# Gathering layer 1's target rows in layer 1's own stage, and reading the edge lists first

## The reference

```python
h = jnp.maximum(_layernorm(x, axis=-1), 0.0)
x = x + _L0_gnn_ref(h, src, dst, ...)   # three mean-aggregating layers
...                                     # then L1, L2 and L3 in the same form

def _sage_mean(h, src, dst, inv_deg, W_neigh, W_self, b_self):
    neigh_sum = jax.ops.segment_sum(h[src], dst, num_segments=h.shape[0])
    return h @ W_self.T + b_self + (neigh_sum * inv_deg) @ W_neigh.T
```

## Time and profile before

| | us |
|---|---|
| median of 3 executions (5771.94 to 5776.87) | 5776.05 |
| the profiled execution | 5786.49 |
| its span (first to last instruction) | 5784.8 |
| setup, up to the stage "positions" | 0 to 203.5 |
| "positions" and "lookup" | 203.5 to 738.6 |
| stage A | 738.6 to 1289.5 |
| stage B1 | 1289.5 to 1462.3 |

### The profile page before, as it was taken

How to read it: one execution, slowest core, us unless ns; L and a number is a source line. 1 busy time by engine, 2 the same in 40 slices (tenths; PEclk the granted TensorE clock), 3 DMA queues, 4 the chain that set the end, 5 groups by cost and what they waited for, 6 DMA issues and landing times. The chain is left out here.

```text
span 5784.8 us, 105438 instructions
## 1 busy us (share of the span) xinstructions
PE 4497.3 (78%) x24851; PEld 3351.3 (58%) x24851; DVE 3664.0 (63%) x13925; ACT 2760.9 (48%) x6045; POOL 3556.8 (61%) x3609
## 2 busy tenths in 40 slices
PE   2897946669998998635767746999999898776774
PEld 1575734447786687534655534666666685443774
DVE  4897845546775787744358737899999403443652
ACT  0497945543783585533211100888888422222431
POOL 0477767740660471075767750888888675777687
PEclk9998967779999999955989879999999757888887
DMA  3365656659888887844677769888898434443564
GB/s 107 118 217 165 202 173 207 209 170 317 271 276 267 280 289 260 281 150 154 231 219 157 141 117 265 274 283 284 283 285 284 139 116 146 142 147 114 133 117 64
DMA packets 726797, 1164.91 MB, mean 201 GB/s; under 512 B 104781, under 2 KB 387647, under 8 KB 726270
## 3 DMA queue, kind: packets, MB, share of 16 engines
q1 hardware_dynamic: 556220, 936.12, 50.0%
q0 software_dynamic: 134400, 161.92, 13.7%
q10 hardware_dynamic: 36000, 64.94, 3.0%
HBM read 638.98 MB, written 545.66 MB: 205 GB/s over the span
## 5 line engine op out<-in xcount | busy, mean ns | idle before, releaser
L1080 POOL DMA_INDIRECT G_V<-layer_rows,i_tb x400 | 379.9, 950 | 576.7 <-POOLq L257 431.1
L1104 PE MATMUL bank<-first_last_indicators,G_V 125*128 (+1 forms) x1600 | 267.4, 289 | 180.5 <-DVE G_V L1739 180.5
L2521 POOL TENSOR_TENSOR P_gA<-P_x,bn_scale 128x512 f32<-128x512 f32 x196 | 250.8, 1280 | 227.1 <-DMA P_x<-node_table 203.1
L1912 POOL DMA_INDIRECT node_table<-H_out,H_rows_of_src x200 | 326.1, 1631 | 101.8 <-issue 55.5
L1912 POOL DMA_INDIRECT out<-O_out,i_srcf x200 | 320.7, 1603 | 101.6 <-issue 55.7
L1080 POOL DMA_INDIRECT G_x<-node_table,i_src x200 | 192.8, 964 | 306.4 <-POOLq L257 245.7
L1104 PEld LDWEIGHTS bank<-first_last_indicators,G_V 125*128 125x128 f32 x1600 | 271.3, 256 | 184.6 <-issue 129.9
L2602 ACT ACTIVATE P_xh<-P_xh,P_nb,P_rs 128x128 f32<-128x128 f32 x784 | 320.2, 479 | 0.0
L1444 PE MATMUL bank<-B_S,B_V 127*128 127x125 f32 x2000 | 279.6, 285 | 47.5 <-DVE B_S L1420 37.8
L1008 POOL DMA_INDIRECT degree_and_position<-es_posf,es_i_position x200 | 197.2, 986 | 179.2 <-DMA dst_keys<-dst_keys 118.6
L1444 PEld LDWEIGHTS bank<-B_S,B_V 127*128 127x128 f32 x2000 | 255.6, 199 | 59.3 <-issue 49.1
(11 more groups left out here) (465 smaller groups left out, 14184.3 us busy)
## 6 DMA issues: line engine op xcount, KB each, us to landing
P_x<-node_table SPq DMA_DIRECT2D x196, 512.0 KB
x_and_h<-P_xh SPq DMA_DIRECT2D x195, 512.0 KB
B_V<-values SPq DMA_DIRECT2D x250, 256.0 KB, 2.7
BN_g<-node_table SPq DMA_DIRECT2D x195, 256.0 KB
out<-P_out SPq DMA_DIRECT2D x195, 256.0 KB
node_table<-G_xg SPq DMA_DIRECT2D x97, 512.0 KB
values<-G_V SPq DMA_DIRECT2D x150, 256.0 KB
layer_rows<-A_a SPq DMA_DIRECT2D x100, 256.0 KB, 3.3
```

What stands on the lines that cost most here:

```text
L1080: pool.indirect_dma_start(out=rows[u][:, c, :], out_offset=None, in_=table, in_offset=index_of(index, i, c)).then_inc(landed[u], 16)
L1104: last = nc.tensor.matmul(m.bank[7][:, bass.ds((i * TILE + c) * 2, 2)], V[0:EP, c, :], m.ind[0:EP, bass.ds(i * TILE + c, 1), :].rearrange( ...
L1912: pool.indirect_dma_start(out=table, out_offset=index_of(index, i, c), in_=out[u][:, c, :], in_offset=None, bounds_check=table.shape[0] - ...
L2521: nc.gpsimd.tensor_tensor(t[v % 2][:], x[v][:, :, D:2 * D], m.Arow[:].unsqueeze(1).to_broadcast([128, TILE, D]), ALU.mult)\
```

## The change

```diff
-def key_row(nc, m, f, i, bank, s_row, s_sel):
+def key_row(nc, m, f, i, bank, s_row, s_sel, behind=2):
...
-        f.after(s_sel, i - 2)
+        f.after(s_sel, i - behind)
...
+def first_layer(nc, m, a):
...
+            @block.gpsimd
+            def _(pool):
+                def body(i, u, f):
+                    f.after(s_h, i - 4)
+                    f.landed(s_xo, i - 4, u)
+                    gather(pool, f, m.i_dst, i, u, a["x"], xd_whole, s_g)
...
+            @block.vector
+            def _(dve):
+                def body(i, u, has):
+                    f = Flow(dve, has)
+                    if has(i):
+                        f.landed(s_g, i, u, 64)
+                        ln.stats(dve, f, i, u, [xd[u][:, c, :] for c in range(TILE)])
+                    if has(i - 1):
+                        ln.finish(f, i - 1, (u - 1) % 4)
+                        row_selectors(nc, m, f, i - 1, (u - 1) % 4, bK, S, s_row, s_sel, s_agg)
+                    if has(i - 4):
+                        f.after(s_T, i - 4)
+                        f.landed(s_ro, i - 8, u)
+                        nc.vector.tensor_copy(rows[u][:], bR[u % 2][0:EP, :].rearrange("p (c f) -> p c f", c=TILE)).then_inc(s_r, 1)
...
+            @block.tensor
+            def _(pe):
+                def body(i, u, has):
+                    f = Flow(pe, has)
+                    key_row(nc, m, f, i, bK, s_row, s_sel, behind=1)
+                    if has(i - 2):
+                        v = (u - 2) % 4
+                        f.after(s_h, i - 2)
+                        f.after(s_hdT, i - 3)
+                        for c in range(TILE):
+                            last = nc.tensor.transpose(bH[:, c * EP:(c + 1) * EP], hd[v][:, c, :], m.ident[0:EP, 0:EP])
+                        last.then_inc(s_hT, 1)
+                        f.after(s_ac, i - 4)
+                        add_up(nc, m, f, i - 2, v, V, S, bA[v % 2], s_V, s_sel, s_agg)
+                    if has(i - 4):
+                        f.after(s_o, i - 4)
+                        f.after(s_r, i - 6)
+                        for c in range(TILE):
+                            last = nc.tensor.transpose(bR[u % 2][0:EP, c * D:(c + 1) * D], o[u][:, c * EP:(c + 1) * EP], m.ident[:])
+                        last.then_inc(s_T, 1)
+                    if has(i - 3):
+                        v = (u - 3) % 4
+                        f.after(s_hdT, i - 3)
+                        f.after(s_ac, i - 3)
+                        f.after(s_o, i - 5)
+                        nc.tensor.matmul(bM[v % 2][:, 0:EG], m.w["self1"], hdT[v][:], start=True, stop=False)
+                        nc.tensor.matmul(bM[v % 2][:, 0:EG], m.w["neigh1"], agg[v][:], start=False, stop=True).then_inc(s_m, 1)
+
+                sweep(pe, 0, n, n + 3, body, back=6, ahead=0, special=0)
+
...
-        layer(nc, m, 1, m.HDa, m.HDb, m.TB1[0:m.T * 128, :])
+        first_layer(nc, m, a)
```

More of the change, by code:

```diff
@@ L604, in _ @@
                 sp.dma_start(b[:], a["dst"][SPAN - 1:SPAN - 1 + (EP - 1) * SPAN].rearrange("(p t) -> p t", t=SPAN)[:, 0:2]).then_inc(s_d, 16)
-                for k in ("dst", "src", "edge_type_9"):
-                    sp.dma_start(m.edge[k].rearrange("(p t) -> p t", p=EP), a[k].rearrange("(p t) -> p t", p=EP)).then_inc(s_c, 16)
-                for k in range(COPIES):
-                    r = slice(k * E // COPIES, (k + 1) * E // COPIES)
-                    sp.dma_start(m.edge["ea"][r, :], a["edge_attr_128"][r, :]).then_inc(m.s_ea, 16)
-                sp.dma_start(m.edge["ea"][E:, :], a["edge_attr_128"][0:128 - EP, :]).then_inc(m.s_ea, 16)
-                sp.wait_ge(s_c, 48)
+                lists.sources(sp, a)
+                sp.wait_ge(lists.s_prev, 1)
+                lists.load(sp, a)
+            @block.scalar
+            def _(act):
+                weights.load(act)
+            @block.gpsimd
+            def _(pool):
+                nc.gpsimd.memset(lists.rows[3][0][0:1, :], -1).then_inc(lists.s_prev, 1)
+                weights.constants(pool)
             @block.vector
@@ L625, in _ @@
             def _(pe):
+                pe.wait_ge(weights.s_ms, 6)
                 pe.wait_ge(s_v, 3)
@@ L752, in edges_setup @@
     m.KT = nc.dram_tensor("keys_type", [T, EP], F32, kind="Internal").ap()
+def edges_setup(nc, m, a, weights, lists):
+    N, E = m.N, m.E
+    T = E // EP
+    TC = T // 2
+    LOW = 256
+    NH = -(-N // (2 * LOW)) * 2
+    BIG = float(1 << 22)
     gathers, scatters = (m.i_src, m.i_dst, m.i_src2, m.i_tb), (m.i_dstf, m.i_srcf)
@@ L760, in sb @@
         return keep.enter_context(nc.sbuf_tensor("es_" + name, shape, dt))
-    ri = [[sb(f"r_{k}{c}", [TC, EP], I32) for c in range(2)] for k in ("dst", "src", "typ", "prev")]
+    ri = lists.rows
     rf = [[sb(f"f_{k}{c}", [TC, EP]) for c in range(2)] for k in ("dst", "src", "typ", "prev")]
@@ L961, in edges_setup @@
-    s_oh, s_hm, s_c, s_16 = m.sem("es_onehot"), m.sem("es_hist"), m.sem("es_chain"), m.sem("es_iota16")
-    with nc.Block() as block:
-        @block.vector
-        def _(dve):
-            def body(i, u, has):
-                f = Flow(dve, has)
-                p = u % 2
-                f.after(s_hm, i - 2)
-                for c in range(TILE):
-                    t = bass.ds(i * TILE + c, 1)
-                    nc.vector.tensor_scalar(oh_lo[p][:, c, :], io_lo16[0:EP, :], lo_f[:, t], None, ALU.is_equal)
-                    last = nc.vector.tensor_scalar(oh_hi[p][:, c, :], io_hi16[0:EP, :], hi_f[:, t], None, ALU.is_equal)
-                last.then_inc(s_oh, 1)
-            nc.vector.tensor_copy(io_lo16[:], io_lo[:]).then_inc(s_16, 1)
-            nc.vector.tensor_copy(io_hi16[:], io_hi[:]).then_inc(s_16, 1)
-            dve.wait_ge(s_16, 2)
-            sweep(dve, 0, n, n - 1, body, back=4, ahead=0, special=0)
+            sweep(dve, EARLY, n, n - 1, count, back=EARLY - 1, ahead=0, special=0)
@@ L986, in _, with count @@
         def _(pe):
-            def body(i, u, has):
+            def count(i, u, has):
                 f = Flow(pe, has)
@@ L1062, in edges_setup @@
     keep.close()
+    lists.stack.close()
+    weights.early.close()
 def every(pool, n, body):
```

540 lines of the change are left out of this document (327 added, 213 removed).

## The result

The changed kernel takes 5644.21 us (median of 4 executions, 5638.06 to 5645.48) against 5773.99 us for the kernel before (5768.26 to 5776.87): a ratio of 0.9773, interval 0.976 to 0.9786, 129.8 us less. Forecast were 5673 us, 103 less, with a range of 5600 to 5765; it lay 29 us too high.

What follows compares the result with a forecast made beforehand. Bounds: the setup's chain waiting behind SP's queue, POOL's gathers in stage A, PE in B1. Setup -53.5, A -236 and B1 +187 sum to -103, giving 5673 us, range 5600 to 5765.

Steps and rivals of the forecast that it cites:

- the lists ahead of `edge_attr`: Setup: the lists no longer wait behind `edge_attr` on SP's queue; 203.5 us falls to 150, gain 53, range 45 to 60.
- POOL's four gathers less in A with the PE and ACT loop next: Stage A: POOL's pace falls to 5.0 us, the PE-ACT loop gives 5.15 a pass; 550.9 us becomes 315, -236.
- the loop between DVE and PE in B1: Stage B1: DVE's 3.7 us and PE's 2.3 add up in each pass; 172.8 us becomes 359.4, +187.
- B1 at full clock: Rival for B1: full clock throughout, passes of 6.05 us, B1 332 us, total 5646 us; chance 0.20.
- The two ends of the sum: B1's pass: 6.05 us at full clock, 8.2 at half clock, where PE's part doubles to about 4.5 us.
- The middle: B1's clock taken as 0.84, between 0.72 and 0.96, giving a pass of 6.6 us.
- The setup's start: Setup: DVE's chain starts near 28.8 us instead of 80.69; a start later than 30 would show the prediction wrong.
- The rule on the clock: B1: the skill says long waits between matmul bursts throttle PE; read as short, B1's gap would leave the pass at 6.05.
- Slower with both stages at half clock: Rival for A and B1: half clock in both, A 450 us, B1 438, total 5887 us; chance 0.10.
- B1 at half clock throughout: Rival for B1: passes of 8.2 us, B1 438 us, +265, total 5752 us; chance 0.12.
- POOL's pace in B1: Rival for B1: DVE-PE loop hidden, gathers set passes of 5.0 us, B1 281 us, total 5594; chance 0.06.
- No gain in the setup: Rival for the setup: the chain's start hangs on something other than SP's queue, total 5726 us; chance 0.06.

## Why the prediction was right

- **Mechanism.** All three stages moved the way they were forecast and by the mechanism named: the lists ahead of `edge_attr`, POOL's four gathers less in A with the PE and ACT loop next, the loop between DVE and PE in B1. The total of the rival "B1 at full clock" (5646) lies nearer to the measured 5644, but its mechanism did not happen: B1's clock was 0.87, between the forecast's bounds of 0.72 and 0.96, and its pass 6.51 us against the forecast's 6.6.
- **B1's pass.** The two ends of the sum were 6.05 and 8.2 us; the passes are 5.98 at full clock, and 7.6 to 7.8 where PE's part, near half clock, took 3.8 us and not 4.5. The middle was chosen, not known; the two-pass alternation was not foreseen, and that its mean came within 0.1 us of the forecast is in part luck.
- **The 29 us** by which the forecast lay too high are for the larger part terms at the ends of stages. In A the forecast had 260 us from the first statistics to the last, 49 passes of 5.15 and 8 for a slow start. Measured are 253.8: the first six passes take 5.78 us on average, so the slow start is there, but costs about 4 us, and the others take 5.09. The tail from the last statistics (948.25 to 989.5) is 41.2 us instead of the 47.6 read before; together that makes A 12.6 us better. In B1 the drain behind the last statistics took 22.8 us, not 29 (its passes hold no new group, 3.15 to 3.44 us each, where I took 6), and the passes 4.4 us less: 11. The setup was 4.5 us worse: the chain ended at 70.1 and not between 63 and 69, and what comes behind it took 84.4 us instead of 82.5. The chain ended late because it started late (next point); its 37.5 us lie within the 34 to 40 of the forecast. POOL's work beside it was costed at next to nothing, with the chain named as its cover; yet it is the chain that it slows down, which ended 4.6 us earlier without a part of it. Of the rest 2.4 us lie in "positions" and "lookup", some 6 behind B1, and 2 in the median of before, now 5773.99.
- **The setup's start.** 18.6 for ACT's issues, 2.8 for the flag and 7.1 for `edge_attr` gave a start at 28.8. DVE's first instruction in the block does begin at 28.1, but the cast that the forecast counted from (80.69 before) begins at 32.62: that is later than 30 us, one of the prediction's own signs of being wrong. The cause is not the queue or the flag. The sum left out that DVE has 4.5 us of instructions ahead of that cast, most of them for the early groups of the histogram; of its 1.7 us before, none counted, since they ran ahead of the wait for the lists.
- **The rule on the clock.** The Trainium skill ("TensorE: Matmul & The Clock Gate", section "HAM oscillation — how this bites in real kernels"), as the prediction read it, would have let B1's gaps pass as short, with 6.05 us for all passes. The trace does not agree with that reading: with gaps of 2.15 to 2.28 us the clock went down in every second pass, and filling them brought it back to 0.96. The section behind it, "A second HAM failure mode: psum-queue depth-cycling", has it that frequent short idle times between groups of matmuls let the clock go up and down too; that is what these rows show.
- **The rivals.** Slower with both stages at half clock: A's clock was 0.91, its mean pass 5.18, as the row at full clock had it and not the one at half. B1 at half clock throughout: its passes took turns between the two levels and took 6.51 us on average, not 8.2. POOL's pace in B1 became true only when the loop was cut. No gain in the setup: it gained 49.

## What to carry to other kernels

When work moves from one stage to another, cost each stage by its own slowest loop, and look for waits that two engines have for each other within one pass: here one instruction at the head of PE's pass made DVE's 3.7 us and PE's 2.3 us add up, and moving it behind the instructions that don't need its input gave 74 us, the steadier clock included. A move off the critical path can also leave idle time in PE, and that has a price of its own in the clock. Ends of stages (start and drain) were the larger part of the error, so read them from rows rather than from the length of a pass. And when an edit is meant to bring back one stall, read every queue in its trace: here a run meant to show SP's queue was decided by ACT's.

## What the runs showed of the hardware

- TensorE's clock can alternate with the passes of a loop: with about 2.2 us of idle time in every pass of 6 us, passes of 5.98 us (granted clock 1.00) and 7.6 to 7.8 us (0.55 for the first 3.8 us) took turns for some 35 passes, and in the same way in three other kernels with this stage.
- The copies issued on one queue can hold up the issue on another: beside the 12.8 MB of `edge_attr` copies that SP had issued, three weight DMAs held ACT's queue for 22.30 us, and for 1.42 us where the copies came later.
- Idle work can pay: 100 products of 128x500 more, with 200 more matmul instructions, made the stage 21 to 25 us shorter by holding the clock at 0.96.
- POOL's selects and DVE's one-hots slow each other: 1.2 us for a select beside DVE against 0.6 alone, and one-hots of 0.69 to 1.64 us against 0.28 to 0.31.
